# A fused adaLN block on one core: a shorter warm-up and another order of the steps for x's second half

## The reference

```
mod = silu(c) @ wmod                      # six rows of 256 per batch
sa, ca, ga, sb, cb, gb = mod              # shift, scale, gate; twice
ga, gb = sign * max(|.|, 0.25)
h = layernorm(x) * (1 + ca) + sa
Q, K, V = split(h @ c_attn_w + c_attn_b)  # one head of width 256
A0 = softmax(Q[:128] K[:128]^T * s)       # s = 1/4, the first 128 of the width
cam = tanh((A0 @ V[:128]) * cam_gate) @ K[:128]^T * (s * layer_weight)
x = x + ga * (softmax(Q K^T * s + cam) @ V @ c_proj_w + c_proj_b)
h = layernorm(x) * (1 + cb) + sb
x = x + gb * (gelu(h @ proj1^T + b1) @ proj2^T + b2)
```

## Time and profile before

| what | value |
|---|---|
| median of 3 runs | 322.36 us (322.35 to 322.36) |
| profiled execution, its own time | 322.67 us |
| span of the profiled execution | 320.9 us |
| granted TensorE clock, mean | 1.00 |
| PE busy | 313.8 us (98%) |
| DVE busy | 214.3 us (67%) |
| ACT busy | 157.6 us (49%) |
| POOL busy | 108.5 us (34%) |

### The profile page before, as it was taken

The page is one execution under the profiler, slowest core; times in us unless marked ns, Lnnn a source line. Parts: engine busy times, 40 slices in busy tenths (PEclk is TensorE's granted clock), DMA queues, the critical chain, the costliest instruction groups (busy, mean ns, idle before and its releaser), DMA issues.

```text
span 320.9 us, 5227 instructions
## 1 busy us (share of the span) xinstructions
PE 313.8 (98%) x2022; PEld 283.9 (88%) x2022; DVE 214.3 (67%) x415; ACT 157.6 (49%) x266; POOL 108.5 (34%) x131
## 2 busy tenths in 40 slices
PE   8889999999999999999999999999999999999996
PEld 6778989888999998898899888898999999899895
DVE  5695689996555669886743789898664575753531
ACT  2465575563334337816932486545532244860930
POOL 4431755154445656135011132140021232603311
PEclk9999999999999999999999999999999999999999
DMA  7920030600000000000001000000000000001001
GB/s 219 375 64 1 0 67 1 239 24 0 3 0 2 0 2 1 2 33 33 3 22 43 2 1 2 0 2 0 0 2 0 2 0 2 0 3 50 16 7 62
DMA packets 8025, 10.31 MB, mean 32 GB/s; under 512 B 704, under 2 KB 6592, under 8 KB 8000
## 3 DMA queue, kind: packets, MB, share of 16 engines
q1 hardware_dynamic: 8000, 9.98, 9.4%
HBM read 7.35 MB, written 2.10 MB: 29 GB/s over the span
## 4 chain that ended last, share of the span: by engine, by line
PE 86%; DVE 9%; ACT 3%; issue 2%; DVEq 0%
PE a_ps L190 13%; PE a_ps L189 13%; PE a_ps L188 13%; PE s_ps L188 11%; PE s_ps L190 11%; PE s_ps L189 11%; PE t_ps L1096 7%; DVE nmax L750 2%; PE s_ps L938 2%; PE t_ps L1023 2%; DVE k_lo L720 1%; PE s_ps L953 1%; DVE th L732 1%; DVE q_hi L718 1%; ACT prob L524 1%
## 5 line engine op out<-in xcount | busy, mean ns | idle before, releaser
L514 ACT ACTIVATE pt_hi<-t_ps 128x512 fp32r<-128x512 f32 x64 | 35.0, 596 | 67.6 <-PE t_ps L1096 67.5
L750 DVE TENSOR_REDUCE nmax<-s_ps 128x1 f32<-128x1024 f32 x32 | 39.0, 1220 | 14.9 <-PE s_ps L190 14.9
L524 ACT ACTIVATE prob<-s_ps,nmax 128x1024 f32<-128x1024 f32 x32 | 35.8, 1119 | 13.3 <-DVE nmax L750 13.1
L744 DVE TENSOR_TENSOR pt_lo<-t_ps,pt_hi 128x512 fp32r<-128x512 f32 x64 | 40.9, 681 | 1.3 <-ACT pt_hi L514 1.3
L188 PE MATMUL s_ps<-k_hi,q_hi 128*128 128x512 f32 x96 | 38.4, 400 | 0.2 <-DVE k_lo L671 0.2
L344 POOL TENSOR_SCALAR prob<-prob,rinv 128x1024 f32<-128x1024 f32 x16 | 18.0, 1127 | 58.3 <-DVE rinv L754 58.3
L190 PE MATMUL s_ps<-k_hi,q_lo 128*128 128x512 f32 x96 | 37.7, 393 | 0.0
L189 PE MATMUL s_ps<-k_lo,q_hi 128*128 128x512 f32 x96 | 37.5, 391 | 0.0
L188 PE MATMUL a_ps<-v_hi,pt_hi 128*128 128x256 f32 x128 | 36.8, 288 | 0.0
L188 PE MATMUL a_ps<-w_hi,pt_hi 128*128 128x256 f32 x128 | 36.4, 284 | 0.0
L189 PE MATMUL a_ps<-w_lo,pt_hi 128*128 128x256 f32 x128 | 36.2, 283 | 0.0
(11 more groups left out here) (150 smaller groups left out, 760.6 us busy)
## 6 DMA issues: line engine op xcount, KB each, us to landing
w_raw<-w_t SPq DMA_DIRECT2D x2, 1024.0 KB, 6.2
out<-x_all SPq DMA_DIRECT2D x16, 128.0 KB, 1.7
x_all<-x SPq DMA_DIRECT2D x4, 256.0 KB, 4.8
wmod_raw<-wmod SPq DMA_DIRECT2D x1, 1024.0 KB, 8.5
x_all<-x SPq DMA_DIRECT2D x2, 512.0 KB, 10.3
wmod_raw<-wmod SPq DMA_DIRECT2D x1, 512.0 KB, 4.8
wattn_raw<-w_attn SPq DMA_DIRECT2D x1, 512.0 KB, 6.0
gates<-h SPq DMA_DIRECT2D x4, 128.0 KB, 2.6
```

Source lines behind the costliest of these rows:

```text
L514: A(pt_hi[:, (u // 2) % 2, 4 * g:4 * g + 4, (u % 2) * P:(u % 2 + 1) * P], t_bank(b, "p", 2 * u + g)[:, :].rearrange("p (t n) -> p t n", n= ...
L524: A(prob[:, u % 3, :], s_ps[u % 2][:, :], ACT.Exp, bias=nmax[:, u:u + 1], accum_out=rsum[:, u:u + 1]).then_inc(exp_ready, 1)
L744: V.tensor_tensor(pt_lo[dst], t_bank(b, "p", 2 * u + g)[:, :].rearrange("p (t n) -> p t n", n=P), f(pt_hi[dst]), ALU.subtract).then_inc(pt ...
L750: V.tensor_reduce(nmax[:, u:u + 1], s_ps[u % 2][:, :], AX.X, ALU.max, negate=True).then_inc(nmax_ready, 1)
```

## The change

TensorE issues six warm-up matmuls in place of nine, and the memset ahead of them covers the 256 columns that they read, in place of 512. In ScalarE's list the high part of v tile 1 goes behind the high parts of x's second half. In VectorE's list the full values and low parts of x's second half go ahead of the low part of v tile 1, and the low part of k (job 1) goes behind the low parts of v tiles 1 and 2.

```diff
@@ block.scalar
             v_high(0, 0)
             qk_high(1)
-            v_high(0, 1)
             h_high(3)
             h_high(2)
+            v_high(0, 1)
             v_high(0, 2)
@@ block.vector
-            V.memset(f32s[:, 0, :], 0.0).then_inc(warm_ready, 1)
+            V.memset(f32s[:, 0, 0:2 * P], 0.0).then_inc(warm_ready, 1)
@@ block.vector
             qk_low(0)
             v_low(0, 0)
-            qk_low(1)
-            v_low(0, 1)
             h_full(2)
             h_full(3)
             h_low(3)
             h_low(2)
+            v_low(0, 1)
             v_low(0, 2)
+            qk_low(1)
@@ block.tensor
-            warm_up(9)
+            warm_up(6)
             modulation(0)
```

## The result

The changed kernel takes 324.11 us (median of 20 runs, 322.2 to 326.36) against 322.49 us (321.68 to 323.38) for the kernel before beside it: a ratio of 1.0054, 95% interval 1.0033 to 1.0076. It is slower by about 1.6 us where 1.7 us of gain was forecast. The profiled execution is the fastest of the 20: 322.2 us, span 320.4, against 322.67 and 320.9 before.

A forecast was written before the change was run, and what follows sets the result against it. TensorE, busy for 98% of the span, was taken as the bound, so only an earlier start of the steady part could pay. Gains of 0.85 + 0.85 = 1.7 us gave 322.36 - 1.7 = 320.66, rounded to 320.7 us, range 320.4 to 322.3.

The forecast's parts named there:

- The sum of 0.85 + 0.85: Start-up: the gains of shorter warm-up and new order add to 1.7 us, carried to the end.
- The clock is lost (slower): Rival, 16%: TensorE falls to 1.2 GHz between warm-up and first half's products, giving 323.3 to 325.9 us.
- the rise at 6.71: Warm-up: the clock steps from 1.2 to 2.4 GHz at 6.71 us, so the three matmuls removed ran fast, about 1.3 us.
- Edit 1: Warm-up of six matmuls and smaller memset: modulation starts once its weights land, gaining 0.85 us, bounds 0.65 to 1.3.
- Edit 2: New ScalarE and VectorE order in x's second half: TensorE resumes at 21.28 instead of 22.16, gaining 0.85 us.
- the full value r=3: VectorE step in x's second half: waits for the high part r=3 at 20.53 and ends at 21.35.
- a margin of 0.1: Second half: low parts are ready 0.1 us before TensorE's second product with one; if not, at most 0.2 lost.
- The k low part of job 1: VectorE before the first scores: delay costs nothing while 0.3 us hold; running late there would lose 0.7 us.
- Carried to the end: Whole kernel: the 1.7 us won in the start-up shortens the total by as much.
- that rival: Rival, 5%: a limit with a fixed origin in the steady part swallows the start-up gain, leaving 322.3 us, within 0.2%.

The follow-up runs named there:

- six_plus_hole2: Changed kernel plus two matmuls of zeros behind the transposes of x's first half, where TensorE waits: 322.37 us, ratio 0.9991, clock held in 3 of 12.
- order_nine: Changed kernel with nine warm-up matmuls and the full memset again, so only the new order differs from the kernel before: 322.20 us, ratio 0.9993.
- nine_hole2: Changed kernel with nine warm-up matmuls and two matmuls of zeros behind the first transposes: 321.45 us, ratio 0.9973, held in 12 of 12.
- eight_hole2: Changed kernel with eight warm-up matmuls and two matmuls of zeros behind the first transposes: 321.43 us, ratio 0.9975, held in 12 of 12.
- seven_hole2: Changed kernel with seven warm-up matmuls and two matmuls of zeros behind the first transposes: 321.16 us, ratio 0.9962, held in 10 of 12.
- six_only: Kernel before with six warm-up matmuls and the 256-column memset, old order kept: 324.43 us, ratio 1.0069, held in 0 of 12.
- seven_hole2_old: Changed kernel with seven warm-up matmuls, two matmuls behind the first transposes and the old order of x's second half: 321.99 us, ratio 1.0004.
- order_eight: Changed kernel with eight warm-up matmuls in place of six: 321.76 us, ratio 0.9979, clock held in 7 of 12.

## Why the prediction was wrong, point by point

- **The failed step is the clock, which the sum put at nothing.** The sum of 0.85 + 0.85 takes the modulation, the transposes and the first half's products at their old lengths. By their mean clock all 20 executions had about 3 to 10 us at 0.50, and in the profiled one they lie from the end of the first transposes to just before the fold. Against the 321.1 us of the changed start-up with the clock held (`six_plus_hole2`, three executions on another chip) that costs about 3.0 us at the median, more than both gains. The rival "The clock is lost (slower)", 16%, was the case, and its number held: 323.3 was given, 324.1 measured, inside its 323.3 to 325.9. What failed is the chance. I argued that the rise at 6.71 left just the remaining records ahead of it and that 3.6 us of the same weak work had not brought the clock down. Both came from one profiled execution. The kernel before loses the clock as well, in 9 of 35 executions on one chip, so it already stood at the edge; its three runs that I was shown agreed within 0.01 us and told nothing of that. With six and nothing in the hole the edge is crossed every time: 0 of 20 and 0 of 12 held. That the rival's number fits is in part luck: it charged 2.65 us, half of a stretch as long as the first rise took (5.3 us), while the low stretches were about 3, 7 and 10 us long, and in the profiled execution 3.4 us of low clock lost 1.2 us up to the fold.
- **The rise is not at 6.71 in general.** The premise that exactly three warm-up matmuls run at the full clock holds for the profiled execution alone. `order_nine` has the same instructions up to there: its warm-up records start 0.43 us apart up to 4.58 and 0.22 apart from 4.82 on, and its modulation starts at 6.98 instead of 8.01. Where the clock rises early, nine are done when the weights come, and edit 1 has little to win; where it rises late, 0.85 or more. So the mean gain of edit 1 with the clock held should be smaller than the 0.85 of the sum: held medians of `nine_hole2`, `eight_hole2` and `seven_hole2` are 321.45, 321.43 and 321.12, the first on another chip than the other two.
- **How many records run at the full clock does not decide either.** In the changed kernel's trace all 12 warm-up records are slow; in `six_only` the last three are fast (from 5.14), and it loses the clock all the same, and earlier. In `seven_hole2_old` all 14 ahead of the modulation are slow (nine in a row cover 4.04 us, 0.43 apart), and the clock holds. The records of line 938 in the changed kernel (shortest, median and longest in ns), then rows of the timelines of `six_only` and `seven_hole2_old`:

```profile
L938 PE MATMUL s_ps<-f32s x12: 634/634/792, 1.2 to 6.0; 128*128 128x256 f32 x12
```

```profile
5.14 0.81 PE L938 MATMUL s_ps<-f32s 128*128 128x256 f32 x3
```

```profile
3.46 4.04 PE L938 MATMUL s_ps<-f32s 128*128 128x256 f32 x9
```

- **Edit 1, 0.85 us up to the first product**: measured 0.97 in the profiled execution, whose weights let the modulation start at 6.83 instead of 7.0. Right in size, for that execution, in which load and first matmul start together at 6.83 (I had allowed 0.1 us between them). The memset went from 0.48 to 0.27 and bought nothing, as said: the warm-up starts 0.26 us earlier and ends in a wait of 0.18 us for the weights.
- **The step beside GpSimd was missed.** I never set GpSimd's subtraction against VectorE's 4-column step. It cost the first product only 0.1 us. That step came 1.06 us earlier (10.09 to 9.03), the subtraction only 0.56 (9.56 to 9.00), so it had just begun and VectorE sat through its 0.73 us; ScalarE's affine began at 9.85, 0.13 after the last transpose (8.65 + 1.07). The Trainium skill (SBUF — State Buffer, Who interferes with whom) says that in its two-port modes VectorE contends with GpSimd, and that whoever issues first blocks the other for the whole instruction. The trace agrees: 9.00 + 0.73 and 9.03 + 0.72 end together within 0.02 us, and where the step comes first it takes 0.17. Even before, the two ended within 0.03 us of each other (9.56 + 0.73 and 10.09 + 0.23), which the timeline could have told me.
- **Edit 2, 0.85 us**: 0.6 by the traces. The first part of the term was right: TensorE goes on with the second half's products 2.57 us after the transposes' start (21.51 - 18.94) in place of 3.48. The failing term is the full value r=3. I let it start practically at once after the high part it waits for; it starts 0.20 after (21.00 against 20.02 + 0.78), and 0.20 also in the traces of `order_nine`, `eight_hole2` and `seven_hole2`. The same handover in the first half takes 0.13 us in the kernel before (11.73 against 10.82 + 0.78), so at least that much could have been read. The low parts come 0.2 later, and the second product with a low part, for which I had found a margin of 0.1, waits: in the chain the second record of line 962 carries 0.51 us where the first carries 0.24, so 0.27 are lost there. I had named this point and allowed 0.2 for it. The k low part of job 1, the other risk, was done at 24.66 (23.98 + 0.68), before job 2's could start.
- **"Carried to the end"** held: 26.20 to 320.9 is 294.7 us before, 25.84 to 320.4 is 294.6 after. Nothing later swallowed the start, so that rival fell.

What stays open: why the full value r=3 starts 0.20 us after its releaser, where the first half's takes 0.13, and what exactly about the stretch lets the clock go. That two more in front help is shown (0 of 32 with six, 7 of 12 with eight), and that one in front beats one in the middle on one chip; that the 2-column matmuls count for little is only argued. No run separates the work in front from the wait for the weights that follows a short warm-up (0.18 us in the changed kernel, 0.85 in `six_only`).

## What to carry to other kernels

A warm-up is not paid off when the clock has risen: the amount of it also decides in how many executions the clock survives the next stretch of small matmuls and waits, and here that could not be read from one trace. Before shortening one, count in how many executions the clock stays up, over 10 or more, because one profile shows one draw. Idle TensorE time that is bound by another engine is a place for matmuls of zeros at no cost that these runs could see: eight in front and two there held the clock in 12 of 12 and gave 0.8 us (seven and two 1.2 us, with less certainty of the clock), where six in front alone had lost 1.6.

## What the runs showed of the hardware that was not expected

The moment of the first rise varies between executions of the same instructions: nine warm-up matmuls had ended and the modulation began at 6.98 us in one (`order_nine`) and at 8.01 in another (the kernel before). At 1.00 of granted clock in the profile's rows the warm-up records can still be 0.43 us apart (in the kernel before until 6.71); only a later fall is shown as 0.50. And times fall in groups by mean clock: in the changed kernel 0.995, 0.989 and 0.984 lie about 1.6 us apart. Elsewhere the distances differ: the kernel before on one chip has medians of 322.46 when held, 323.38 at 0.995 and 326.42 at 0.989, `order_eight` 321.12, 322.73 and 325.46.
